# TensorE's order within a slot: the down product moved ahead of projection pieces and values

## What is computed

```
x = x + layernorm(attention(layernorm(x), W_qkv, W_out, b_out))
x = x + layernorm(ffn(layernorm(x), W_up, W_gate, W_down))

attention: 16 heads of 32, rotary q and k, key j seen by query i if i - 128 <= j <= i,
           softmax, values, then W_out and b_out
ffn:       w -> ternary: scale = mean(|w|) + 1e-8, clip(round(w / scale), -1, 1) * scale
           hidden = silu(x @ up.T) * (x @ gate.T)      (2048 wide)
           out = hidden @ down.T
```

## Time and profile before

| what | value |
|---|---|
| median of 3 runs | 1500.68 us (1498.4 to 1501.43) |
| the profiled execution | 1500.58 us, its span 1498.8 us |
| TensorE matmul busy | 1347.8 us, 90% |
| VectorE, ScalarE, GpSimd busy | 962.3, 758.6, 668.5 us |
| granted TensorE clock, mean | 0.98 of full speed |
| share of TensorE in the chain that ended last | 15% of the span (the chain is followed back through part of the run only) |

### The profile page before, as it was taken

One profiled execution on the slowest core, in us unless ns is written; L12 is line 12 of the kernel. 1 busy time (PEld: TensorE's weight loads), 2 busy tenths in 40 slices (PEclk: granted clock), 3 DMA queues, 4 the chain that ended last, 5 costly groups with the idle time before them and its releaser, 6 DMA issues. The chain is left out here.

```text
span 1498.8 us, 28511 instructions
## 1 busy us (share of the span) xinstructions
PE 1347.8 (90%) x10246; PEld 949.7 (63%) x10246; DVE 962.3 (64%) x2460; ACT 758.6 (51%) x1473; POOL 668.5 (45%) x907
## 2 busy tenths in 40 slices
PE   5686777799899999999899999999899999899997
PEld 3464554476666766667666766667666767666775
DVE  3578998986575756666575756666665657533332
ACT  2585554455554555555554555555454546432432
POOL 2432333544374544544374544544364544244433
PEclk9897999999999999999999999999999999999999
DMA  5677644553474535754574635754463535300000
GB/s 191 192 213 224 189 134 134 147 113 82 109 148 96 131 76 106 146 120 103 101 155 85 143 76 105 147 111 106 99 132 87 142 69 121 69 29 15 15 1 29
DMA packets 306445, 168.22 MB, mean 112 GB/s; under 512 B 227968, under 2 KB 281600, under 8 KB 306304
## 3 DMA queue, kind: packets, MB, share of 16 engines
q1 hardware_dynamic: 306304, 166.39, 46.9%
HBM read 84.48 MB, written 25.17 MB: 73 GB/s over the span
## 5 line engine op out<-in xcount | busy, mean ns | idle before, releaser
L711 ACT ACTIVATE prob<-prob,peak 128x256 f32<-128x256 f32 x512 | 229.8, 498 | 73.8 <-DVE peak L921 73.8
L1220 PE MATMUL Y<-down_q,room 128*128 128x512 fp8e4 x1024 | 262.3, 379 | 1.0 <-POOL room L621 1.0
L1143 PE MATMUL J<-xnT,W 128*128 128x512 f32 x512 | 251.5, 617 | 10.3 <-ACT xnT L695 10.3
L979 DVE SCALAR_TENSOR_TENSOR room<-room,J 128x512 f32<-128x512 f32 x113 | 77.8, 688 | 240.5 <-ACT room L763 240.4
L921 DVE CUSTOM_DVE_ANT_0 prob<-S,band,neg_score_scale 128x256 f32<-128x256 f32 x512 | 225.5, 478 | 9.2 <-PE S L1084 5.4
L609 POOL TENSOR_TENSOR o_n<-o_raw,rinv 128x128 f32<-128x128 f32 x128 | 53.7, 420 | 389.2 <-DVE rinv L950 389.2
L1205 PE MATMUL J<-xT_hi,up_q 128*128 128x256 f16 x904 | 203.6, 273 | 18.6 <-DVE xT_lo L971 18.6
L1205 PE MATMUL J<-xT_hi,gate_q 128*128 128x256 f16 x848 | 191.1, 273 | 19.5 <-DVE xT_lo L971 17.3
L763 ACT ACTIVATE room<-J,sig_scale 128x512 f32<-128x512 f32 x113 | 77.5, 686 | 249.5 <-PE J L1205 249.5
L1205 PE MATMUL J<-xT_lo,up_q 128*128 128x256 f16 x904 | 203.5, 273 | 0.0
L1205 PE MATMUL J<-xT_lo,gate_q 128*128 128x256 f16 x848 | 190.9, 273 | 0.0
(11 more groups left out here) (128 smaller groups left out, 2512.0 us busy)
## 6 DMA issues: line engine op xcount, KB each, us to landing
spill<-split SPq DMA_DIRECT2D x64, 256.0 KB, 2.7
Qp<-spill SPq DMA_DIRECT2D x128, 128.0 KB, 2.9
Kp<-spill SPq DMA_DIRECT2D x128, 128.0 KB, 3.0
x_in<-in_x SPq DMA_DIRECT2D x32, 256.0 KB, 4.0
room<-in_w_up SPq DMA_DIRECT2D x16, 512.0 KB, 6.4
room<-in_w_gate SPq DMA_DIRECT2D x16, 512.0 KB, 4.3
room<-in_w_down SPq DMA_DIRECT2D x16, 512.0 KB, 5.0
X<-in_x SPq DMA_DIRECT2D x32, 256.0 KB, 3.0
```

The lines of the kernel that those rows point to most:

```text
L711: e = nc.scalar.activation(prob[:, U % PROBS, a, :], prob[:, U % PROBS, a, :], ACT.Exp, bias=peak[:, U % PROBS, a:a + 1], scale=-1.0)
L979: nc.vector.scalar_tensor_tensor(sig[:, q % 2, :], sig[:, q % 2, :], 1.0, FF_ps[FF_BANK[FF_NUMBER[("U", q)]]][:], ALU.add, ALU.mult).then_ ...
L1143: e = pe.matmul(dst[:], W[:, part, c, g * P:(g + 1) * P], xnT[:, c, :], start=(c == 0), stop=(c == DC - 1))
L1220: e = pe.matmul(Y_ps[t][:], h[:, q % HELD, part, (a * HT + t) * P:(a * HT + t + 1) * P], down_q[:, 2 * pair + a, :], start=(pair == 0 and ...
```

## The change

Within a slot, TensorE takes `down` directly behind `score`, ahead of `fill` and `weighted_values`, instead of behind them. `ff_work` (FT, up, gate) stays last. No other engine's order, no wait and no instruction is changed.

```diff
@@ -1236,13 +1236,13 @@
                     transpose_probs(s - 1)
                 if s + 2 < ALL_UNITS:
                     score(s + 2)
+                q, t = divmod(s - FF_FIRST, 2)
+                if 0 <= q - DOWN_LAG < ALL_PAIRS:
+                    down(q - DOWN_LAG, t)
                 for kind, g, tile, chunks in pieces_at(s):
                     fill(kind, g, tile, chunks)
                 if 0 <= s - LAG < ALL_UNITS:
                     weighted_values(s - LAG)
-                q, t = divmod(s - FF_FIRST, 2)
-                if 0 <= q - DOWN_LAG < ALL_PAIRS:
-                    down(q - DOWN_LAG, t)
                 for job in ff_jobs_at(s):
                     ff_work(job)
```

## The result

| | median | runs |
|---|---|---|
| before | 1501.06 us | 1498.4 to 1501.77, 4 runs |
| changed | 1510.14 us | 1508.88 to 1512.75, 4 runs |

A forecast was written before the change was run, and what follows sets the result against it. TensorE, busy 90% of the span, bounds the kernel, so only waits can change its time. Terms 4.3 + 0.86 - 1.95 + 1.8 + 0.2 + 0.4 = +5.6 us on 1500.68 gave 1506.3 us; range 1502.0 to 1511.0.

The forecast's parts named there:

- ordinary slots: Slots outside the named places, such as one with a Q piece and gate product: down first costs 0.
- Position 31 and slot 254: Last slot of each 32-slot tile: V0's delay passes through ScalarE's list, +0.86 us, five times; slot 254 behind OT, +0.86.
- Position 19: Slot 19 of each 32-slot tile: ScalarE copies V3 late anyway, so gate starts 0.39 us earlier, five times, -1.95.
- Position 23: Slot 23 of a tile: Q0's delay two slots earlier reaches gate through GpSimd, ScalarE, VectorE; +0.45 us, four times, +1.8.
- Slots 243 to 247: The last V3 piece pushes a chain to gate once: +0.2 us, at least 0, at most 0.86.
- Position 30: Slot 30 of each tile: OT copies and p_low delay VectorE's half of FT's copy, 0 to +0.15 us, five times, +0.4.
- The size of the move: Down's four matmuls delay pieces and values by 0.86 us, 215 ns each; the skill's 131 ns would give 0.52.
- high ends: Slots at tile positions 23 and 30 and slots 243 to 247 at 0.67, 0.24 and 0.86 us: sum +7.9.
- rival (c): More: moved VectorE and GpSimd work collides at tile positions 19, 23, 30, 31, +4 us on top, 1510.5 us; chance 0.13.
- (a): Only a wash: tile position 31 costs 0.43 each, position 23 is covered; +1.5, 1502.2 us; chance 0.13.
- (b): Faster: ScalarE comes late to pieces everywhere; tile positions 31, 23 and slot 254 cost nothing; -1.95, 1498.7 us; chance 0.05.
- (d): Down at the slot's head waits for hidden's low half in many slots; needs GpSimd 2.7 us later; chance below 0.01.

The follow-up runs named there:

- position 21 undone: Changed kernel with down back behind pieces and values at position 21 of each 32-slot tile only: 1510.33 us, ratio 1.0065 to before.
- position 31 alone: Kernel before with down first only at position 31 of each 32-slot tile and in slot 254: 1509.38 us, ratio 1.0049 to before.
- filled kernel: Changed kernel with 14 unneeded matmuls between FT and gate at position 31 of each tile (slots 95 to 223): 1507.56 us, ratio 1.0035 to before.

## Why the prediction was right or wrong

**What bounds the kernel, and that ordinary slots don't move.** Right. Outside the places named, and apart from what a half-clock stretch left over to the next slot, slots kept their length to 0.03 us, and down's wait stayed as it was (1.0 us, once).

**Position 31 and slot 254.** Right in place, mechanism and size of the wait (0.79 and 0.86 for 0.86; at 31 the V piece itself took 2.84 us instead of 2.90). Moving FT's copy ahead in the lists removed it, undoing the order there removed it.

**Position 19.** Right to 0.01 us.

**Position 23.** The chain was the right one, its price 0.52 for 0.45, and it has five slots, not four: slot 87 was left out of the count.

**Slots 243 to 247.** Right chain, mis-sized: 0.9 for 0.2. I let the masks of slot 244 swallow part of the delay; statistics and hidden stood behind it in VectorE's list as well, and up in slot 244 itself waited 0.3 longer. The upper end, 0.86, was the measure.

**Position 30.** +0.25 for +0.4, but not for the reason given. GpSimd's add moved by 0.86 as well, so p_low lost as much time to it as before: in all ten cases, five in each trace, p_low ended 0.55 us after the add, and its length is the same in both kernels, 1.11 and 1.12 us in slot 158, 0.82 to 0.83 in the other four. I had read slot 158 alone, and it is the exception: in the four others VectorE had about 0.3 us more slack before FT's half, and the 0.86 showed as 0.03, while in 158 it showed as 0.13. That p_low is blocked again is what the prediction took from the Trainium skill, SBUF — State Buffer, SBUF: two separate sides, and the traces agree with it in all ten; the price of 0.15 that the prediction gave for that case fits 158 alone (0.13). No run tested the port lock as the cause.

**What was missing.** The sum had no term for the clock. The step that failed is the one that priced a wait by its own length: at position 31 and in slot 254 a wait grew beyond 2 us, and in four of six cases most or all of the 16 matmuls behind it ran at 1.2 GHz, 1.5 to 1.7 us more. In the profiled execution that is 6.4 of 11.6 us. All the rest made 5.2, for which 5.6 had been forecast: the places of the sum came to 6.6, and small gains that were not forecast took 1.3 off. In before's rows the clock was 1.00 behind each wait of 1.4 to 1.8 us, so the trace could not give a price; but in the first 300 us, with their longer waits, the granted clock is below full speed, and that was a row to bound it from. These are the pages of before and of after (tenths of full speed in 40 slices of the span):

```profile
PEclk9897999999999999999999999999999999999999
...
PEclk9898999999999999999999999999999999999999
```

**Luck.** The sum's own terms, all at their high ends, reached +7.9, 1508.6 us; the measured 1510.14 lies in the range because that took in rival (c) and the spread of three runs. The direction and the places were reasoned; that the range held is in part luck.

Rival (c), a collision of VectorE and GpSimd, reached a similar total for a reason that did not act where it was placed: at positions 19, 23, 30 and 31 p_low kept its length to 0.02 us. Collisions did move elsewhere: at positions 2, 22 and 28 p_low grew from 0.87 to 1.55 us, 15 times, at 14 it shrank from 1.24 to 0.69 and at 25 from 1.56 to 0.90. All these lie under cover: the slots at 2, 14, 25 and 28 kept their length to 0.03 us and those at 22 became 0.06 shorter. Rivals (a), (b) and (d) did not occur.

**The size of the move.** Down's four matmuls take 1.03 us from first start to last end again, and the shift measured in slot 254 is 0.86: the 215 ns of the trace hold. By the Trainium skill, TensorE: Matmul & The Clock Gate, Back-to-back issue gap, the shift would have been an estimated 0.52 us, and the measurement decides against it; what the same section gives for an isolated matmul of 512 columns, about 216 ns, is what this stream shows.

## What to carry to other kernels

When work is moved ahead in one engine's order, go through everything that it delays by who stands behind it in the next engine's list: nothing changes where cover is left, and the price appears whole where an engine was idle for just that input. Look then at how long the longest waits of TensorE become: a wait that grows from 1.4 to 2.2 us may cost the clock for what follows, 1.5 to 1.7 us here, twice what the wait grew by. And a block of work is worth moving into a wait that is bare; here moving the same 0.86 us of down cost 9 us with FT last in its slot and gained 19 us with FT early; and with only FT's copies moved ahead in the lists the kernel was as fast as before.

## What the hardware showed that was not expected

- The granted clock fell to 0.50 behind waits of 2.2 to 2.6 us in 11 of 19 cases behind slot 64 (changed kernel 4 of 6, position 21 undone 5 of 6, position 31 alone 1 of 6, slot 254 of the filled kernel 1 of 1), and behind the more than 150 waits of 1.4 to 1.8 us in all traces only once (slot 255 above). Filling 1.5 of the 2.2 us with matmuls that nobody needs left it at 1.00 in all five. No experiment here varied what decides between two equal waits, such as those of slots 127 and 159: it stays open.
- A float32 piece behind a score of four short matmuls became 0.06 us shorter when down came between, 17 times. That its weight loads now lie behind down is the likely reason and was not tested. It also happens inside longer slots, such as 151, whose K piece reads, before and after:

```profile
761.79 1.94 PE L1143 MATMUL J<-xnT,W 128*128 128x512 f32 x4
```

```profile
763.55 1.88 PE L1143 MATMUL J<-xnT,W 128*128 128x512 f32 x4
```
